# Attention of a Mamba/MoE block chain: maximum and exponential two query tiles ahead, swaps and roundings a step later, probabilities and values in two rounded parts

## What is computed

```python
qs = (x @ wq_sem); ksem = (x @ wk_sem)                  # 16 heads x 64
qg = _rope(x @ wq_geo); kg = _rope(x @ wk_geo)          # 16 heads x 64
v = (x @ wv).reshape(b, sl, H, DV)                      # 16 heads x 128
g = sigmoid(gate_logit)
scores = g * sem_scores + (1.0 - g) * geo_scores        # each scaled by 1/8
attn = softmax(where(causal, scores, NEG_INF))
out = einsum('bhqk,bkhd->bqhd', attn, v).reshape(b, sl, H * DV) @ wo
```

## Time and profile before

| | |
|---|---|
| median of 3 runs | 1935.2 us (1932.26 to 1939.66) |
| the profiled execution | 1957.88 us, its span 1956.3 us |
| TensorE busy | 1752.7 us, 90% of the span |
| VectorE, ScalarE, GpSimd busy | 1136.6, 1026.0, 803.0 us |
| granted TensorE clock over the span | 0.958 |
| first and last transpose of probabilities (L906) start | 447.2 and 1493.6 us |

### The profile page before, as it was taken

How to read it: one execution, slowest core, us unless ns; L and a number is a source line. 1 busy time by engine, 2 the same in 40 slices (tenths; PEclk the granted TensorE clock), 3 DMA queues, 4 the chain that set the end, 5 groups by cost and what they waited for, 6 DMA issues and landing times. The chain is left out here.

```text
span 1956.3 us, 34013 instructions
## 1 busy us (share of the span) xinstructions
PE 1752.7 (90%) x9530; PEld 1375.0 (70%) x9530; DVE 1136.6 (58%) x2173; ACT 1026.0 (52%) x2244; POOL 803.0 (41%) x788
## 2 busy tenths in 40 slices
PE   6399989338999999999999999999997999999998
PEld 2255656327878888788788788888886766666777
DVE  4799953695665565655555555556563333333567
ACT  4599923015656566666666565656564334443322
POOL 1489931423344444344434343444441233212354
PEclk9699999568999999999999999999999999999989
DMA  4742348200000000000000000000103999999623
GB/s 138 291 182 102 102 149 268 88 0 17 20 20 7 25 14 11 19 17 22 14 11 19 19 6 24 14 24 8 41 6 99 284 308 310 304 308 300 180 88 96
DMA packets 100409, 193.36 MB, mean 99 GB/s; under 512 B 15460, under 2 KB 59748, under 8 KB 97748
## 3 DMA queue, kind: packets, MB, share of 16 engines
q1 hardware_dynamic: 58836, 108.76, 18.2%
q0 software_dynamic: 17152, 47.67, 7.7%
q10 hardware_dynamic: 24336, 35.98, 5.6%
HBM read 140.84 MB, written 51.51 MB: 98 GB/s over the span
## 5 line engine op out<-in xcount | busy, mean ns | idle before, releaser
L1196 POOL TENSOR_TENSOR sw<-sw,rope_t 64x512 f32<-64x512 f32 x128 | 164.1, 1282 | 594.3 <-ACT sw L1006 594.3
L916 PE MATMUL ps<-pt,v 128*128 128x256 f32 (+1 forms) x1280 | 278.8, 365 | 8.1 <-DVE v L1085 7.1
L998 ACT ACTIVATE pb<-ps,negmax 128x128 f32<-128x128 f32 (+7 forms) x256 | 190.6, 744 | 146.7 <-DVE negmax L1069 146.6
L916 PEld LDWEIGHTS ps<-pt,v 128*128 128x128 f32 x1280 | 234.1, 191 | 37.2 <-issue 7.1
L985 ACT COPY pt<-ps 128x512 f32<-128x512 f32 (+3 forms) x384 | 171.3, 481 | 83.7 <-PE ps L906 70.3
L906 PE MATMUL ps<-ident,pb 128*128 128x128 f32 x1152 | 173.0, 277 | 46.1 <-ACT pb L998 44.9
L550 POOL DMA_DIRECT2D w2r<-in_w x148 | 77.2, 522 | 333.2 <-PE ps L599 289.3
L1199 POOL TENSOR_TENSOR t<-t,sw 64x512 f32<-64x512 f32 x128 | 185.7, 1451 | 32.7 <-POOL sw L1196 16.0
L906 PEld LDWEIGHTS ps<-ident,pb 128*128 128x128 f32 x1152 | 132.4, 141 | 85.6 <-ACT pb L998 33.1
L1069 DVE TENSOR_REDUCE negmax<-ps 128x1 f32<-128x128 f32 (+7 forms) x256 | 191.4, 748 | 0.0
L633 DVE SCALAR_TENSOR_TENSOR ga<-th,ps 128x176 f32<-128x176 f32 x148 | 50.0, 338 | 241.3 <-ACT th L614 241.3
(11 more groups left out here) (206 smaller groups left out, 4055.7 us busy)
## 6 DMA issues: line engine op xcount, KB each, us to landing
w13r<-in_w SPq DMA_DIRECT2D x124, 352.0 KB, 6.5
w2r<-in_w POOLq DMA_DIRECT2D x148, 176.0 KB, 6.5
result<-yy ACTq DMA_DIRECT2D x148, 128.0 KB, 5.5
crow<-c_rows SPq DMA_DIRECT2D x32, 512.0 KB, 3.6
t<-sorted SPq DMA_DIRECT2D x124, 128.0 KB, 5.8
sorted<-zeros ACTq DMA_DIRECT2D x15, 1024.0 KB, 17.0
hc<-in_w SPq DMA_DIRECT2D x24, 352.0 KB, 6.0
wraw<-in_wqk SPq DMA_DIRECT2D x16, 256.0 KB, 2.7
```

Source lines behind the costliest of these rows:

```text
L916: last = pe.matmul(ps[:, 6, c0:2 * P], v[:, j, hd], pt[g % 2][:, j, c0:2 * P], start=j == 0, stop=j == 2 * g + 1)
L998: act.activation(pb[:, qt % 2, 0:cols], ps[:, bank:bank + 2, :].rearrange("p a n -> p (a n)")[:, 0:cols], ACT.Exp, bias=negmax[:, par, qn: ...
L1196: g.tensor_tensor(sw[64:128, p % 2, :], sw[64:128, p % 2, :], rope_t[64:128, 1, (p // 2) * 512:(p // 2 + 1) * 512], ALU.mult).then_inc(s_t ...
```

## The change

Four things. (1) v becomes vr and vl, pt becomes ptr and ptl, and `output` on TensorE calls `three`. ScalarE rounds (ptr, vr), VectorE subtracts (ptl, vl). `s_pl` and, for values, `s_e7` are now counted by those subtractions. (2) `max_tile` and `exp_tile` are of tile qt + 2 instead of qt + 1. (3) `swap`, `turned` and `values` of a fill are taken in the step after the fill, behind that step's `probs`; `rounded` and `rest` two steps after the fill. (4) The last fills of values come a step group earlier and pieces have other steps: 2, 3, 6, 7 in the even head and 1, 2, 3, 5 in the odd one (before: 2, 3, 5, 6 in both). The `add_out` calls stand first in steps 4, 6, 0 and 2 (before: within steps 3, 5, 7 and 1). The diff, cut:

```diff
         pb = sbo("pb", [P, 2, SEQ])
-        v = sbo("v", [P, 8, 2 * P])
-        pt = [sbo("pt0", [P, 6, 2 * P]), sbo("pt1", [P, 8, 2 * P])]
+        vr = sbo("vr", [P, 8, 2 * P], F32R)
+        vl = sbo("vl", [P, 8, 2 * P], F32R)
+        ptr = [sbo("ptr0", [P, 6, 2 * P], F32R), sbo("ptr1", [P, 8, 2 * P], F32R)]
+        ptl = [sbo("ptl0", [P, 6, 2 * P], F32R), sbo("ptl1", [P, 8, 2 * P], F32R)]
...
-        V01, V23, Q0, K0, V45, Q1, K1_, V67 = range(8)
+        V01, V23, Q0, K0, V45, V67, Q1, K1_ = range(8)
...
-        PIECE = {2: 0, 3: 1, 5: 2, 6: 3}
-        VALUE = {0: 0, 1: 1, 4: 2, 7: 3}
+        PIECE = ({2: 0, 3: 1, 6: 2, 7: 3}, {1: 0, 2: 1, 3: 2, 5: 3})
+        VALUE = {0: 0, 1: 1, 4: 2, 5: 3}
+
+        def piece_at(hh, qt):
+
+            return PIECE[hh].get(qt)
+
+        def value_at(hh, qt):
+
+            return VALUE.get(qt) if hh == 0 else None
...
-                    last = pe.matmul(ps[:, 6, c0:2 * P], v[:, j, hd], pt[g % 2][:, j, c0:2 * P], start=j == 0, stop=j == 2 * g + 1)
+                    last = three(pe, ps[:, 6, c0:2 * P], vr[:, j, hd], vl[:, j, hd], ptr[g % 2][:, j, c0:2 * P], ptl[g % 2][:, j, c0:2 * P],
+                                 j == 0, j == 2 * g + 1)
...
-                    act.copy(pt[g % 2][:, j0:j1, cols], ps[:, 4 + ci % 2, 0:(j1 - j0) * P].rearrange("p (j q) -> p j q", q=P)).then_inc(s_pl, 1)
+                    act.copy(ptr[g % 2][:, j0:j1, cols], ps[:, 4 + ci % 2, 0:(j1 - j0) * P].rearrange("p (j q) -> p j q", q=P)).then_inc(s_pr, 1)
...
+            def values(m, fill):
+                act.wait_ge(s_b7, fill)
+                act.copy(vr[:, 2 * m:2 * m + 2, :].rearrange("p i d -> p (i d)"), ps[:, 7, :]).then_inc(s_vr, 1)
...
             exp_tile(0, 0, 0)
+            exp_tile(0, 1, 0)
...
                 for qt in range(8):
                     probs(it, qt)
-                    if qt < 7 or not last:
-                        exp_tile(it, qt + 1, hh)
+                    swapped = piece_at(hh, qt - 1)
+                    if swapped is not None and not last:
+                        swap(n0 + swapped, swapped, piece_fill(pair, hh, swapped))
+                    if qt == 0 and hh == 1:
+                        swap(4 * it + 3, 3, piece_fill(pair, 0, 3))
+                    taken = value_at(hh, qt - 1)
+                    if taken is not None:
+                        values(taken, value_fill(pair, taken))
                     if qt == 0 and not first(it):
                         output(it - 1, 3)
                     if qt in (2, 4, 6):
                         output(it, qt // 2 - 1)
-                    if qt in PIECE and not last:
-                        p = PIECE[qt]
-                        swap(n0 + p, p, piece_fill(pair, hh, p))
-                    if qt in (3, 4, 6, 7) and not last:
-                        p = {3: 0, 4: 1, 6: 2, 7: 3}[qt]
-                        rounded(n0 + p, p, 1 - hh)
+                    if qt < 6 or not last:
+                        exp_tile(it, qt + 2, hh)
+                    turned_before = piece_at(hh, qt - 2)
+                    if turned_before is not None and not last:
+                        rounded(n0 + turned_before, turned_before, 1 - hh)
+                    if qt < 2 and hh == 1:
+                        rounded(4 * it + 2 + qt, 2 + qt, 1)
...
+            def probs(it, qt):
+
+                for ci, j0, j1 in chunks(qt):
+                    dve.wait_ge(s_pr, CHUNKS * it + ci + 1)
+                    g = qt // 2
+                    o = (slice(None), slice(j0, j1), slice((qt % 2) * P, (qt % 2 + 1) * P))
+                    dve.tensor_tensor(ptl[g % 2][o], ps[:, 4 + ci % 2, 0:(j1 - j0) * P].rearrange("p (j q) -> p j q", q=P),
+                                      ptr[g % 2][o].bitcast(F32), ALU.subtract).then_inc(s_pl, 1)
...
-            def values(m, fill):
-                dve.wait_ge(s_b7, fill)
-                dve.tensor_copy(v[:, 2 * m:2 * m + 2, :].rearrange("p i d -> p (i d)"), ps[:, 7, :]).then_inc(s_e7, 1)
+            def values(m, n):
+                dve.wait_ge(s_vr, n)
+                o = vr[:, 2 * m:2 * m + 2, :].rearrange("p i d -> p (i d)")
+                dve.tensor_tensor(vl[:, 2 * m:2 * m + 2, :].rearrange("p i d -> p (i d)"), ps[:, 7, :], o.bitcast(F32), ALU.subtract).then_inc(s_e7, 1)
...
                 for qt in range(8):
-                    if qt < 7 or not last:
-                        max_tile(it, qt + 1, hh)
                     if qt == 0 and not first(it):
-                        rest(n0 - 1, 3, hh)
-                    if qt in (4, 5, 7) and not last:
-                        p = {4: 0, 5: 1, 7: 2}[qt]
-                        rest(n0 + p, p, 1 - hh)
+                        add_out(it - 1, 2, prev_b, 1 - hh)
+                    if qt == 2 and not first(it):
+                        add_out(it - 1, 3, prev_b, 1 - hh)
+                    if qt in (4, 6):
+                        add_out(it, qt // 2 - 2, b, hh)
+                    probs(it, qt)
+                    turning = piece_at(hh, qt - 1)
+                    if turning is not None and not last:
+                        turned(n0 + turning, turning)
+                    if qt == 0 and hh == 1:
+                        turned(4 * it + 3, 3)
+                    taken = value_at(hh, qt - 1)
+                    if taken is not None:
+                        values(taken, 4 * pair + taken + 1)
+                    if qt < 6 or not last:
+                        max_tile(it, qt + 2, hh)
                     if qt == 0 and not first(it):
                         output(it - 1, 3)
-                    if qt == 1 and not first(it):
-                        add_out(it - 1, 3, prev_b, 1 - hh)
...
-                    if qt in (3, 5, 7):
-                        add_out(it, qt // 2 - 1, b, hh)
-                    if qt in VALUE and hh == 0:
-                        values(VALUE[qt], value_fill(pair, VALUE[qt]))
-                    if qt in PIECE and not last:
-                        p = PIECE[qt]
-                        turned(n0 + p, p)
+                    resting = piece_at(hh, qt - 2)
+                    if resting is not None and not last:
+                        rest(n0 + resting, resting, 1 - hh)
+                    if qt < 2 and hh == 1:
+                        rest(4 * it + 2 + qt, 2 + qt, 1)
...
             heads_loop(dve, body)
+            add_out(ITS - 1, 2, 1, 1)
```

More of the change, by code:

```diff
@@ L352, in build @@
         s_T = sem("probs_transposed")
-        s_pl = sem("probs_copied")
+        s_pr = sem("probs_rounded")
+        s_pl = sem("probs_split")
         s_b6 = sem("bank6_filled")
@@ L358, in build @@
         s_a7 = sem("bank7_swapped")
+        s_vr = sem("values_rounded")
         s_e7 = sem("bank7_taken")
@@ L965, in body @@
                         values(VALUE[qt], b, value_fill(pair, VALUE[qt]))
-                    if qt in PIECE and not last:
-                        p = PIECE[qt]
-                        if qt == 2 and next_b == 0:
+                    if qt in PIECE[hh] and not last:
+                        p = PIECE[hh][qt]
+                        if p == 0 and next_b == 0:
                             pe.wait_ge(s_ws, 2 * hp + c // 3 * 2 + (1 - hh) + 1)
@@ L1143, in att_dve @@
             max_tile(0, 0, 0)
+            max_tile(0, 1, 0)
             def body(hp, c, last):
@@ L1176, in body @@
                     if qt == 1 and c == 3 and not last_pair(hp):
-                        dve.wait_ge(s_b7, first_fill(pair, V67))
+                        dve.wait_ge(s_b7, first_fill(pair, K1_))
                         split_qk(2 * hp + 3, 1)
```

## The result

The changed kernel takes 2202.8 us (median of 4 runs, 2199.2 to 2207.5) against 1937.4 us of the kernel before on the same chip: a ratio of 1.137, 95% interval 1.133 to 1.141. It is 265 us slower. The forecast was 2157 us, with 222 us of loss. The profiled execution took 2204.7 us.

What follows compares the result with a forecast made beforehand. TensorE was taken to bound attention; its 61.8 us plus stalls 7.4 + 3.9 + 4.9 + 2.2 gave 80.2 us a pair against 66.3, 222 us over 16 pairs, so 2157 us. Range 1945 to 2260, the likeliest case's own 2040 to 2240.

Steps and rivals of the forecast that it cites:

- Coupled queues: Likeliest case: attention's in-order queues delay releases, stalls (a) to (d) add up; 2157 us, range 2040 to 2240, chance 0.52.
- TensorE's own run: TensorE's work for a pair of heads in attention, without stalls: 63.2 - 1.4 = 61.8 us.
- (a): Bank 6: outputs wait for add_out, behind VectorE's previous step; 8.8 us chain against 5.4 of work; 7.4 us a pair.
- (d): VectorE's splits of the next weights stand in front of the next add_out: 2.2 us a pair.
- (b): Q/K too late: scores of tile 4 and the next head's tile 0 wait for split pieces; 3.9 us a pair.
- (c): Bank 7: fills wait because it is taken after the next step's transposes and copies; 4.9 us a pair.
- the clock falls as well: Rival: TensorE's clock in attention also drops, to 0.8, adding 80 us; time 2237 us, chance 0.05.
- The saving: Products of probabilities and values in rounded parts on TensorE: 0.7 us a head saved, 22 us in all.
- Only the direct handshakes: Rival: (a) and (d) mostly absorbed, (b) and (c) remain in attention; 1942 to 2040 us, chance 0.25.
- TensorE stays the bound: Rival: attention's stalls hidden, waits for the exponential go, 61.8 us a pair; 1863 to 1925 us, chance 0.13.

Runs made afterwards that it cites:

- Run 10: Changed kernel plus 12 unread 512-column matmuls ahead of the two longest-waiting outputs (even head's step 0, odd head's step 6): 2162 us, ratio 1.114.
- run 11: Kernel before with twelve already met waits after each transposes on TensorE, 192 more instructions in the loop body: 1976 us, ratio 1.018.
- run 9: Run 8 without VectorE's subtractions of the probabilities; the third matmul reads the rounded part again: 1932 us, ratio 0.997.
- run 1: Changed kernel with each add_out back at the end of its odd step, ahead of rest: 2107 us, ratio 1.086.
- runs 3: Changed kernel with add_out at the end of its odd step, rounding ahead of the exponential and rest ahead of the maximum: 2109 us, ratio 1.089.
- run 5: Run 4 with add_out at the end of its odd step, rounding ahead of the exponential, rest ahead of the maximum: 2080 us, ratio 1.068.
- run 6: Kernel before with only the maximum and the exponential two tiles ahead: 1930 us, ratio 0.995.
- run 8: Kernel before with two tiles ahead and two parts, subtraction ahead of the maximum, all else in its old steps: 2080 us, ratio 1.073.
- run 4: Changed kernel without the two parts of probabilities and values (copies and plain 32-bit products), new order of work kept: 2116 us, ratio 1.091.
- run 7: Kernel before with only the two parts of probabilities and values, subtraction behind the next tile's maximum on VectorE: 2009 us, ratio 1.037.

## Why the prediction was right, and where it was not

**Direction and mechanism.** "Coupled queues" was the forecast, and the lines of its chain stand in the trace one behind the other. In us a pair (the waits of four heads, halved):

| term | forecast | measured |
|---|---|---|
| TensorE's own run | 61.8 | 67.5 busy |
| (a) bank 6 and (d) weight splits: wait for xr | 7.4 + 2.2 | 6.9 |
| (b) Q/K too late: wait for qkl | 3.9 | 2.75 |
| (c) bank 7: waits for t and vl | 4.9 | 3.8 |
| stops for instructions | none | 2.55 |
| sum, with 0.2 of small waits | 80.2 | 83.7 |

17.4 us a pair times 16 would be 278 us; the runs differ by 265, among other things because the stops for instructions come in five of the eight groups of four heads, this one among them.

**What was mis-sized.** The stalls (a) to (d) were put 5 us a pair too high, 18.4 against 13.4. Of these 5, 1.4 is the wait at the third head's step 0, in whose place the stops for instructions stand here. Two things that the sum did not have, 8.25 us a pair, make up for it, so that 80.2 comes near 83.7 is in part luck. First, TensorE's run: 61.8 was at the full clock. I gave the falling clock a chance of 0.05 and argued that nothing in the rows says that it falls. It did: behind the stall of 3.38 us the matmuls of 256 columns start 0.22 us apart, where they are 0.12 apart ahead of it,

```profile
763.86 0.41 PE L868 MATMUL ps<-ptr,vr 128*128 128x256 f32 x1
764.08 0.41 PE L869 MATMUL ps<-ptr,vl 128*128 128x256 f32 x1
```

and the granted clock of the 3.15 us behind the stall is 0.52, that of the 3 us after them 1.00 (same profile, by stretch, columns as in the earlier trace rows):

```profile
763.05:766.20 3.15, 3.15 (x15) 3.15 (x16) 1.80 (x4) 0.49 (x1) 2.42 (x2) 0.52 0.03 8
766.30:769.30 3.00, 2.52 (x23) 2.27 (x21) 1.72 (x4) 1.70 (x5) 1.97 (x7) 1.00 0.02 5
```

0.52 is the lower of the two levels, 1.2 GHz; the engine had stood idle for 3.38 us before. So the rival "the clock falls as well", 2237 us, came true together with the forecast's chains, and the time lies between the two. Run 10 shows 41 us for two stalls a pair; whether the 80 us that the rival had for all of it is too much or too little is not shown. I read the clock in slices of 49 us, which are averages and hide stretches of 3 us. The Trainium skill ("TensorE: Matmul & The Clock Gate", HAM oscillation) describes short bursts of matmuls between waits, with a fall to the half clock after each longer wait; the trace agrees, with 0.52 behind this one. The granted clock of 0.93 over 167.4 us stands for up to 11.7 us of lost full-clock time, 5.9 a pair, as an estimate; the 5.7 us a pair by which TensorE was busy beyond 61.8 fit into that. How much of them is clock is not settled, since matmuls that start from idle also last longer in the records at the full clock (0.39 against 0.28 us, at 713.97). Second, the loading of instructions, which the change's diff shows as 160 more matmuls in the loop's body and which I did not count at all: 2.55 us a pair in this stretch, 15 us net in the execution (run 11).

**The saving.** The 0.7 us a head by cheaper products is largely borne out: at the full clock the wide products do start 0.12 us apart, and with VectorE out of the way (run 9) four heads are 2.0 us shorter in the loop's first turn, where 2.8 were forecast. The later turns, with the loading of the longer loop, take 22.7 us back.

**The rivals.** "Only the direct handshakes" is refuted by run 1: moving add_out alone brings 96 us. "TensorE stays the bound" needed the chain of (a) under 5.4 us; it was as long as forecast. Where my understanding failed is in the experiments: I held the position of add_out and rest for the cause, and runs 3 and 5 (150 and 110 us above what I expected) show that the lag comes from what fills the queues, that is, from the takes and rotations a step later together with the pieces' new steps (run 5 against run 6: some 140 us) and from the subtractions (run 9 against run 8: 147 us). In the forecast of (a) the subtractions were 1.0 of 8.8 us. The costs do not simply add up: the parts cost 70 us alone, 150 with two tiles ahead (run 8 against run 6) and 87 on top of the whole order (the changed kernel against run 4); the order costs 177 alone. Not tried: the subtraction behind the maximum with two tiles ahead, or behind the swap's rotation; run 7 has the first without two tiles ahead, so that its 70 against 150 may lie in that place too.

## What to carry to other kernels

An engine at 60% of its time can still set the pace if each of its entries is between two others' entries: count the chain from one release to the next through all queues, not the shares. Putting a take of a buffer "a step later" is free only if the shortest step is longer than the chain that follows it. And when work is moved to cheaper instructions of which there are more, look at how long the hardware loop becomes and at what one engine's second look at each tile does to its queue. A mark that recurs in each turn prices such things one by one: runs 6 and 9 differ by 2 us and hid a gain of some 16 and a loss of 23.

## What the runs showed of the hardware

**A longer loop is loaded again.** With 160 more matmuls (or 192 more waits) in TensorE's loop of four heads, its instruction queue moves 77 to 82 packets instead of 30, and TensorE stands still at the start of a turn, in the changed kernel for 2.8 and 2.3 us. The head that holds the stops is longer by 3.0 us in the changed kernel, where other waits are hidden behind them, and by 4.1 to 4.9 us in run 9, where TensorE has little else to wait for. At what length of the body this begins no run shows.

**A cast that waits for GpSimd.** VectorE's rounding of the value weights (128x512, from SBUF to SBUF) took 1.36 us in the mean of 8 in the changed kernel, 1.49 in seven of them and 0.42 in the first. One of the seven, in the timeline:

```profile
736.98 0.69 DVE L1150 TENSOR_TENSOR wl<-wraw,wr 128x512 fp32r<-128x512 f32 x1
...
737.02 1.76 POOL L1239 TENSOR_TENSOR sw<-sw,rope_t 64x512 f32<-64x512 f32 x1 [1.76 <-ACT sw L1019]
...
737.59 1.49 DVE L1154 CAST wvr<-wvraw 128x512 fp32r<-128x512 f32 x1
```

The subtraction began 0.04 us ahead of GpSimd's product, which lasted 1.76 us instead of its usual 1.28; the cast began within it and ended only 0.30 us behind it, at 739.08. In the kernel before the same cast takes 0.42 us, and GpSimd is not at work beside it. The Trainium skill ("SBUF — State Buffer", SBUF: two separate sides) says that VectorE and GpSimd share a pair of ports under an exclusive lock that the one that starts first holds for its whole instruction; on VectorE's side it names instructions with two SBUF inputs, which the subtraction is, and those in a 2-port mode. The trace agrees: the product is 0.48 us longer beside the subtraction, and the cast ends only when the product has. That this cast runs in such a mode no run shows by itself. It is 7.5 us in all (8 times 0.94), and it stands in front of an add_out: the output of the fourth head's step 2 waited 3.26 us (at 740.72), of which these 0.9 us are a part of term (d) that I had not seen.
